# Two norms of eight tiles on GpSimd inside the second attention step, and the last norm's scaling on ScalarE

## The reference

```python
x = x + _L0_gnn_ref(_layernorm(x), adj, ...)
x = x + _L0_ffn_ref(_layernorm(x)[None], ...)[0]
x = x + _L1_gnn_ref(_layernorm(x), adj, ...)
x = x + _L1_ffn_ref(_layernorm(x)[None], ...)[0]

# _L1_gnn_ref: two steps of top-p attention (0.9) and of a fixed graph
for n in range(STEPS):
    A = _top_p_attention(Xa, W1, W2, W3)
    Xf = R @ Xf
    Xa = A @ Xa
    Z = Z + Xf @ U1[n].T + Xa @ U2[n].T
h = X + Z
return (h - mean(h)) / sqrt(var(h) + LN_EPS) * ln_g + ln_b

# _L1_ffn_ref: the routing comes from the mean over all rows, so all rows use the same two experts
logits = mean(x, axis=1) @ Wr + br            # softmax, capacity scale, softmax, top 2, softmax
out = sum over the two experts e of w_e * (gelu(x @ W1[e] + b1[e]) @ W2[e] + b2[e])
return _layer_norm(out + x, gamma, beta)
```

## Time and profile before

| what | value |
| --- | --- |
| median of 3 runs | 904.51 us (904.44 to 907.09) |
| profiled execution | 903.87 us, span 902.1 us |
| VectorE busy | 674.4 us (75%) |
| TensorE busy | 728.7 us (81%) |
| ScalarE busy | 477.1 us (53%) |
| GpSimd busy | 237.0 us (26%) |

### The profile page before, as it was taken

One profiled execution on the slowest core, in us unless ns is written; L12 is line 12 of the kernel. 1 busy time (PEld: TensorE's weight loads), 2 busy tenths in 40 slices (PEclk: granted clock), 3 DMA queues, 4 the chain that ended last, 5 costly groups with the idle time before them and its releaser, 6 DMA issues.

```text
span 902.1 us, 15401 instructions
## 1 busy us (share of the span) xinstructions
PE 728.7 (81%) x5099; PEld 535.5 (59%) x5099; DVE 674.4 (75%) x2305; ACT 477.1 (53%) x707; POOL 237.0 (26%) x489
## 2 busy tenths in 40 slices
PE   4999999859999675999999786967779788775294
PEld 2455555429998443867778476754437576675153
DVE  6758678724444359799871879999899999996768
ACT  4877687115554144465563573849587576602141
POOL 3401330365667007200000142133151341500000
PEclk9999999779999678999999998878788898798588
DMA  8764000076886200000000000000000003001001
GB/s 150 121 94 71 22 22 4 25 214 183 236 234 182 100 1 0 1 2 1 1 2 1 0 2 1 2 1 1 0 1 2 1 2 94 1 1 31 0 4 44
DMA packets 47366, 41.93 MB, mean 46 GB/s; under 512 B 7376, under 2 KB 44112, under 8 KB 47280
## 3 DMA queue, kind: packets, MB, share of 16 engines
q0 software_dynamic: 11456, 14.62, 7.9%
q1 hardware_dynamic: 29488, 19.95, 7.9%
q10 hardware_dynamic: 6336, 6.32, 2.8%
HBM read 39.69 MB, written 9.57 MB: 55 GB/s over the span
## 4 chain that ended last, share of the span: by engine, by line
DVE 37%; PE 17%; issue 5%; ACT 3%; POOLq 1%; DVEq 1%; POOL 1%; ACTq 0%
DVE big L1532 6%; PE bank L1938 4%; PE bank L2033 4%; DVE cand L1451 4%; DVE rm L1306 4%; PE bank L2016 3%; DVE hacc L1446 2%; DVE big L1521 2%; DVE cand L1312 2%; DVE cand L1471 2%; DVE big L1518 2%; DVE top L1466 2%; PE bank L1945 1%; ACT big L1782 1%; PE bank L2195 1%
## 5 line engine op out<-in xcount | busy, mean ns | idle before, releaser
L1782 ACT ACTIVATE big<-bank 128x512 f32<-128x512 f32 x128 | 70.2, 597 | 75.8 <-PE bank L2016 75.8
L2016 PE MATMUL bank<-ident,big 128*128 128x128 f32 x512 | 80.2, 308 | 30.7 <-DVEq L1564 21.4
L1945 PE MATMUL bank<-parts,adjT 128*128 128x128 bf16 x1536 | 92.5, 224 | 5.4 <-DVE xnT L1401 3.4
L1938 PE MATMUL bank<-kk,qq 64*128 64x512 f32 x256 | 78.6, 742 | 21.8 <-ACT big L1752 21.8
L2016 PEld LDWEIGHTS bank<-ident,big 128*128 128x128 f32 x512 | 62.1, 155 | 57.2 <-DVEq L1564 22.5
L1945 PEld LDWEIGHTS bank<-parts,adjT 128*128 128x128 bf16 x1536 | 90.8, 101 | 7.4 <-DVE xnT L1401 3.8
L1752 ACT ACTIVATE big<-bank,negm 128x2048 f32<-128x2048 f32 x32 | 62.6, 1958 | 50.1 <-DVE fsc L1568 40.1
L1532 DVE SCALAR_TENSOR_TENSOR big<-big,st 128x2048 f32<-128x2048 f32 x32 | 75.2, 2388 | 4.8 <-PE bank L2016 4.8
L399 POOL DMA_INDIRECT ys_scratch<-big,parts x62 | 60.0, 967 | 31.5 <-ACT big L759 21.7
L849 PE MATMUL bank<-big,xn 128*128 128x512 f32 x128 | 62.2, 608 | 5.7 <-DVE big L546 5.7
L833 PE MATMUL bank<-xnT 128*128 128x512 f32 x128 | 62.2, 611 | 2.3 <-DVE xnT L535 2.3
(11 more groups left out here) (361 smaller groups left out, 1494.1 us busy)
## 6 DMA issues: line engine op xcount, KB each, us to landing
big<-in_L_ffn_w_dram SPq DMA_DIRECT2D x93, 128.0 KB
big<-in_adj_dram POOLq DMA_DIRECT2D x8, 512.0 KB, 7.5
big<-xs_scratch ACTq DMA_DIRECT2D x31, 132.0 KB
kk<-in_adj_dram POOLq DMA_DIRECT2D x4, 512.0 KB, 8.2
qq<-in_adj_dram POOLq DMA_DIRECT2D x4, 512.0 KB, 10.0
xs_scratch<-hacc SPq DMA_DIRECT2D x9, 132.0 KB
xs_scratch<-hacc ACTq DMA_DIRECT2D x8, 132.0 KB
res<-in_x_dram SPq DMA_DIRECT2D x4, 256.0 KB, 6.9
```

Of the source, the lines that this page charges most:

```text
L1782: nc.scalar.activation(MT[:, 4 * q:4 * q + 4, s * P:(s + 1) * P], bank[:, 5 + q % 2, :].rearrange("p (j i) -> p j i", j=4), ACT.Copy).then ...
L1938: nc.tensor.matmul(bank[:, c, :], qq[lo:lo + DA, (g * G + s) * P:(g * G + s + 1) * P], kk[lo:lo + DA, c * CH:(c + 1) * CH], start=True, st ...
L1945: mm = nc.tensor.matmul(bank[:, b, i * P:(i + 1) * P], adjT[:, jt, t * P:(t + 1) * P], parts[:, k, jt, :], start=(jt == 0 and k == 0), sto ...
L2016: mm = nc.tensor.transpose(bank[:, 5 + q % 2, j * P:(j + 1) * P], mk[:, s, jt * P:(jt + 1) * P], ident[:, :])
```

## The change

- GpSimd gets three helpers. `norm_of` makes mean, variance and inverse root of a slice of tiles, in 21 instructions on 128x4 or 128x8 elements. `first_norm` scales tiles from `h` to `lnu`, multiplies with `lng` and adds into `res`. `second_norm` scales from `res` to `h`.
- They are placed in GpSimd's loop over the groups of the second step: after the search of group 5, `norm_of` and `first_norm` of tiles 0 to 3; after that of group 6, `norm_of` of tiles 0 to 7 (second statistics for 0 to 3, first for 4 to 7) and `first_norm` of 4 to 7; in group 7, `second_norm` of 0 to 3 between the two `after_first`, and after its search `norm_of` and `second_norm` of 4 to 7.
- VectorE takes the statistics of `res` for these tiles with `stats_again` after groups 5 and 6. `two_norms` starts at tile 8 (`EARLY`).
- `lnu` lies in `w_` (`xnT`), not in `mk`; VectorE's wait for all transposes becomes a wait for `less_w` (`sp_done`), the last reader of `w_`. `sums4` gets a buffer of its own.
- TensorE's transposes of the first two quarters of `h` (`turn_h`) and ScalarE's copies of them (`take_h`) move into group 7's round, ahead of the last `flag_sum` and behind the copies of group 6.
- In the last norm ScalarE scales the four tiles of a quarter (Identity with bias and scale), two quarters behind its Gelus. VectorE makes the bias (`nmr`) and does the product with `gam` and the sum into `res` one quarter later (`finish`).

```diff
@@ -1123,15 +1123,17 @@
...
-lnu = mk[:, 1, :].rearrange("p (t d) -> p t d", t=NT)
+lnu = w_
...
-sums4 = r8[:, 8, 2:2 + NC + 1]
+sums4 = sb("sums4", [P, NC + 1])[:, :]
...
 (d_ld, d_ldw, d_xn, d_xT, d_xT_out, d_meanb, d_nm, d_ex, d_w1, d_w2, d_h, d_hid, d_y,
- d_out, d_store) = names("d", "ld", "ldw", "xn", "xT", "xT_out", "meanb", "nm", "ex",
-                         "w1", "w2", "h", "hid", "y", "out", "store")
+ d_out, d_store, d_stat, d_res, d_xn_p, d_nmr, d_yn) = names(
+     "d", "ld", "ldw", "xn", "xT", "xT_out", "meanb", "nm", "ex", "w1", "w2", "h", "hid", "y", "out", "store",
+     "stat", "res", "xn_p", "nmr", "yn")
 FIRST_TILES = (NG - 1) * G
+EARLY = 2 * TPC
@@ -1243,6 +1245,49 @@
...
+        def norm_of(ts):
+            m_, v_, t_, y_, n_ = mean[:, ts], var[:, ts], tmp16[:, ts], rstd[:, ts], newt[:, ts]
+            nc.gpsimd.tensor_tensor(m_, stats[:, ts, 1], stats[:, ts, 4], ALU.add)
+            nc.gpsimd.tensor_tensor(t_, stats[:, ts, 1], stats[:, ts, 4], ALU.subtract)
+            nc.gpsimd.tensor_tensor(v_, stats[:, ts, 2], stats[:, ts, 5], ALU.add)
+            pool.drain()
+            nc.gpsimd.tensor_scalar(m_, m_, 0.5, None, ALU.mult)
+            nc.gpsimd.tensor_scalar(t_, t_, 0.5, None, ALU.mult)
+            nc.gpsimd.tensor_scalar(v_, v_, 1.0 / D, LN_EPS, ALU.mult, ALU.add)
+            pool.drain()
+            nc.gpsimd.tensor_tensor(t_, t_, t_, ALU.mult)
+            pool.drain()
+            nc.gpsimd.tensor_tensor(v_, v_, t_, ALU.add)
+            pool.drain()
+            nc.gpsimd.tensor_scalar(y_.bitcast(I32), v_.bitcast(I32), -0.5, MAGIC, ALU.mult, ALU.add)
+            pool.drain()
+            for _ in range(3):
+                nc.gpsimd.tensor_tensor(n_, v_, y_, ALU.mult)
+                pool.drain()
+                nc.gpsimd.tensor_tensor(n_, n_, y_, ALU.mult)
+                pool.drain()
+                nc.gpsimd.tensor_scalar(n_, n_, -0.5, 1.5, ALU.mult, ALU.add)
+                pool.drain()
+                nc.gpsimd.tensor_tensor(y_, y_, n_, ALU.mult)
+                pool.drain()
+        def first_norm(tiles):
+            for t in tiles:
+                nc.gpsimd.tensor_scalar(lnu[:, t, :], h[:, t, :], mean[:, t:t + 1], rstd[:, t:t + 1],
+                                        ALU.subtract, ALU.mult)
+            pool.drain()
+            for t in tiles:
+                nc.gpsimd.tensor_tensor(lnu[:, t, :], lnu[:, t, :], lng[:, :], ALU.mult)
+            pool.drain()
+            for t in tiles:
+                nc.gpsimd.tensor_tensor(res[:, t, :], res[:, t, :], lnu[:, t, :], ALU.add).then_inc(d_res, 1)
+        def second_norm(tiles):
+            for t in tiles:
+                nc.gpsimd.tensor_scalar(h[:, t, :], res[:, t, :], mean[:, t:t + 1], rstd[:, t:t + 1],
+                                        ALU.subtract, ALU.mult).then_inc(d_xn_p, 1)
         for g in range(NG):
@@ -1251,8 +1296,23 @@
                 continue
             for s in range(G):
                 after_first(g, s)
+                if g == NG - 1 and s == 0:
+                    second_norm(range(0, TPC))
             for s in range(G):
                 after_second(g, s)
+            if g == NG - 3:
+                pool.wait_ge(sp_done, 12)
+                pool.wait_ge(d_stat, TPC)
+                norm_of(slice(0, TPC))
+                first_norm(range(0, TPC))
+            if g == NG - 2:
+                pool.wait_ge(d_stat, 3 * TPC)
+                norm_of(slice(0, EARLY))
+                first_norm(range(TPC, EARLY))
+            if g == NG - 1:
+                pool.wait_ge(d_stat, 4 * TPC)
+                norm_of(slice(TPC, EARLY))
+                second_norm(range(TPC, EARLY))
     @block.vector
@@ -1418,7 +1478,16 @@
             dve.wait_ge(add_done, G * (g + 1))
             dve.wait_ge(rx_added, G * (g + 1))
             for s in range(G):
-                op(nc.vector.bn_stats(stats[:, g * G + s, :], h[:, g * G + s, :]))
+                ins = nc.vector.bn_stats(stats[:, g * G + s, :], h[:, g * G + s, :])
+                if g * G < EARLY:
+                    ins.then_inc(d_stat, 1)
+                else:
+                    op(ins)
+        def stats_again(c):
+            dve.wait_ge(d_res, (c + 1) * TPC)
+            for t in range(c * TPC, (c + 1) * TPC):
+                nc.vector.bn_stats(stats[:, t, :], res[:, t, :]).then_inc(d_stat, 1)
@@ -1613,10 +1682,12 @@
             for k in range(NG - 1):
                 if RXG[k] == g:
                     stats_of(k)
+            if g in (NG - 3, NG - 2):
+                stats_again(g - NG + 3)
         ch.sync()
         dve.wait_ge(c_ldg, 32)
         dve.wait_ge(c_resb, NT)
-        dve.wait_ge(tq_done, 2 * NG * 4 * G)
+        dve.wait_ge(sp_done, 12)
         def two_norms(ts):
@@ -1640,7 +1711,7 @@
                 nc.vector.tensor_scalar(h[:, t, :], res[:, t, :], mean[:, t:t + 1], rstd[:, t:t + 1],
                                         ALU.subtract, ALU.mult).then_inc(d_xn, 1)
-        two_norms(slice(0, FIRST_TILES))
+        two_norms(slice(EARLY, FIRST_TILES))
         add_pv(NG - 1)
         stats_of(NG - 1)
         ch.sync()
@@ -1696,9 +1767,15 @@
...
+        def finish(c):
+            ts = slice(c * TPC, (c + 1) * TPC)
+            dve.wait_ge(d_yn, (c + 1) * TPC)
+            ch.link(nc.vector.tensor_tensor(y[:, ts, :], y[:, ts, :], bcast(gam.unsqueeze(1), [P, TPC, D]),
+                                            ALU.mult))
+            nc.vector.tensor_tensor(res[:, ts, :], res[:, ts, :], y[:, ts, :], ALU.add).then_inc(d_out, 1)
         for c in range(NC):
             ts = slice(c * TPC, (c + 1) * TPC)
-            b3 = [P, TPC, D]
             dve.wait_ge(d_y, c + 1)
@@ -1707,12 +1784,11 @@
             ch.sync()
             mean_var(ch, ts)
             inv_std(ch, ts)
-            for t in range(ts.start, ts.stop):
-                op(nc.vector.tensor_scalar(y[:, t, :], y[:, t, :], mean[:, t:t + 1], rstd[:, t:t + 1],
-                                           ALU.subtract, ALU.mult))
-            ch.sync()
-            ch.link(nc.vector.tensor_tensor(y[:, ts, :], y[:, ts, :], bcast(gam.unsqueeze(1), b3), ALU.mult))
-            nc.vector.tensor_tensor(res[:, ts, :], res[:, ts, :], y[:, ts, :], ALU.add).then_inc(d_out, 1)
+            nc.vector.scalar_tensor_tensor(out=nmr[:, ts], in0=mean[:, ts], scalar=-1.0, in1=rstd[:, ts],
+                                           op0=ALU.mult, op1=ALU.mult).then_inc(d_nmr, 1)
+            if c:
+                finish(c - 1)
+        finish(NC - 1)
...
     @block.scalar
@@ -1846,6 +1922,12 @@
...
+        def take_h(i):
+            a, e = XS[i]
+            act.wait_ge(d_xT, i + 1)
+            nc.scalar.activation(xnT[:, a * P:e * P], bank[:, XB[i], 0:(e - a) * P], ACT.Copy,
+                                 accum_out=sums4[:, i:i + 1]).then_inc(d_xT_out, 1)
@@ -1867,6 +1949,9 @@
             if g:
                 for k in range(4 * G):
                     copy_MT(1, g - 1, k)
+            if g == NG - 1:
+                take_h(0)
+                take_h(1)
             if g + 1 < NG:
@@ -1878,10 +1963,8 @@
                 if g in (2, 3):
                     take_part(g - 2, 1)
                     take_part(g - 2, 2)
-        for i, (a, e) in enumerate(XS):
-            act.wait_ge(d_xT, i + 1)
-            nc.scalar.activation(xnT[:, a * P:e * P], bank[:, XB[i], 0:(e - a) * P], ACT.Copy,
-                                 accum_out=sums4[:, i:i + 1]).then_inc(d_xT_out, 1)
+        for i in range(2, len(XS)):
+            take_h(i)
         act.wait_ge(d_nm, 1)
...
+        def norm(c):
+            act.wait_ge(d_nmr, c + 1)
+            for t in range(c * TPC, (c + 1) * TPC):
+                nc.scalar.activation(y[:, t, :], y[:, t, :], ACT.Identity, bias=nmr[:, t:t + 1],
+                                     scale=rstd[:, t:t + 1]).then_inc(d_yn, 1)
         act.wait_ge(d_w1, 4)
...
                     act.wait_ge(d_y, c - 1)
                 nc.scalar.activation(hid[:, c % 2, u, :], bank[:, v % 4, :], ACT.Gelu,
                                      bias=db1[:, u // HCD, u % HCD:u % HCD + 1]).then_inc(d_hid, 1)
+            if c >= 2:
+                norm(c - 2)
+        for c in range(NC - 2, NC):
+            norm(c)
     @block.tensor
     def _(pe):
@@ -2130,6 +2223,18 @@
...
+        def turn_h(i):
+            a, e = XS[i]
+            if i == len(XS) - 1:
+                pe.wait_ge(add_done, NT)
+            for t in range(a, e):
+                if t < EARLY:
+                    pe.wait_ge(d_xn_p, t + 1)
+                else:
+                    pe.wait_ge(d_xn, t + 1 - EARLY)
+                mm = nc.tensor.transpose(bank[:, XB[i], (t - a) * P:(t - a + 1) * P], h[:, t, :], ident[:, :])
+            mm.then_inc(d_xT, 1)
@@ -2171,16 +2276,15 @@
             for k in range(1, NG, 2):
                 if RXG[k] == g:
                     rx(k)
+            if g == NG - 1:
+                pe.wait_ge(p_ready, 2 * NG * G)
```

(11 more changed lines are left out.)

## The result

The changed kernel took 896.12 us in the median of 4 runs (894.77 to 897.17), beside 904.98 for the kernel before; the ratio is 0.9891 with a 95% interval of 0.987 to 0.9912. It is faster by 1.1%, 8 to 12 us. In a second set of runs, beside others of before, it was 893.86 against 905.36, ratio 0.9884 (0.9861 to 0.9907). Forecast were 893.8 and a range of 890 to 899.

A forecast was written before the change was run, and what follows sets the result against it. The prediction took VectorE, busy 37% of the span, as the bound, with TensorE's products next after group 7. Its terms -13.3 + 1.6 + 1.5 - 0.2 gave -10.4 us: 893.8 us, range 890 to 899.

The forecast's parts named there:

- The end of the second step: Between group 7's end and its `add_pv`, moving tiles 0 to 7 off VectorE removes 13.3 of 26.3 us.
- TensorE is late next: After group 7, VectorE finishes at 826.7 and then waits for TensorE's products, ending at 827.2; 0.5 us of saving is lost.
- `stats_again`, +1.6: After groups 5 and 6, four extra `bn_stats` on VectorE each time, with nothing to hide them, cost 1.6 us.
- VectorE behind GpSimd, +1.5: In the groups, three or four collisions of 0.4 to 0.8 us with GpSimd's large instructions cost VectorE 1.5 us.
- Rival A: GpSimd hardly disturbs VectorE and the search has slack: -11.9 us, giving 892.3; chance 0.20.
- Rival C: `first_norm` instructions over 0.8 us delay GpSimd's threshold search; VectorE waits 2 to 4 us in groups 6 and 7: 896 to 901; chance 0.15.
- cost nothing: Group 7's threshold search starts 4 us late on GpSimd, but 4.3 us of cover and ScalarE absorb it: no cost.
- The early transposes and copies, nothing: Transposes and copies of tiles 0 to 7 fit TensorE's 5.17 us idle before the last flag sum: no cost or gain.
- The last norm, -0.2: In the last two quarters, ScalarE's scaling saves 0.2 us, between -0.6 and +0.6, because TensorE paces the earlier quarters.
- The whole last feed-forward, unchanged in themselves.: Behind `add_pv` of group 7, the routing and last feed-forward keep their lengths and merely come earlier.
- Rival B: GpSimd's added work, 26.6 us, blocks VectorE in full: 918.9 us, slower once over 11.9 us block; chance 0.05.
- rival D: Identity scalings between the Gelus make ScalarE reload its table, two or three exposed loads of 1.3 us: 896.5 to 898; chance 0.07.

The follow-up runs named there:

- after: The changed kernel in its first set of runs and the trace from it; 896.12 us for 904.98 before, ratio 0.9891.
- after_again: The changed kernel run again with no edit, in a second set of runs with its own trace; 893.86 us for 905.36 before, ratio 0.9884.
- skip_third: The changed kernel without VectorE's two norms of tiles 8 to 11 (output wrong there), on another chip; ratio 0.989 to before.
- pool_more: The changed kernel with each of GpSimd's eight first scalings made two more times into unused tiles, on another chip; ratio 0.9963 to before.
- pe_warm: The changed kernel with 36 and 22 unused bf16 products filling two idle stretches of TensorE; ratio 0.9835 to before.
- warm_table2: pe_warm plus one tiny Gelu on ScalarE behind the routing's last Exp; 890.06 us, ratio 0.9834 to before (0.9826 on another chip, as warm_table).
- warm_all: The warm_table2 kernel plus 22 unused bf16 products on TensorE in front of the last flag sum; 890.61 us, ratio 0.985 to before.

## Why the prediction was right, point by point

- **The end of the second step, -13.3 us.** Measured -13.7 (after) and -12.9 (after_again). The step "TensorE is late next" held: skip_third shows VectorE idling for it. It is level with VectorE rather than 0.5 us behind it: before's transposes took 6.35 us up to the product, after's 5.97, after_again's 6.76. What I didn't foresee is that the stretch has two lengths with the clock.
- **`stats_again`, +1.6.** Its rows are 0.86 us for four, 0.77 and 0.77 with overlap. As said, with nothing to hide it.
- **VectorE behind GpSimd, +1.5.** This term was mis-sized: groups 5 to 7 grew by 1.99 us in all, so about 0.45 for the exclusion. I had counted three or four collisions of 0.4 to 0.8 us; there were three larger ones of 0.1 to 0.23. The row that I leaned on, 1.02 us in the earlier trace rows, is one short instruction that started behind a run of additions with no gap and ended with the last of them (365.42 and 365.40 us); here the large instructions fell into MAX8 and MATCH_REPLACE, as the prediction itself said, and pool_more prices such collisions at a tenth of GpSimd's large time. Rival A, without this term, was the better account of the mechanism. Of the signs that I named, the groups' growth of 3 us came out at 2.0 and the single instructions of 0.4 to 1 us didn't come.
- **GpSimd's own time.** The scaling by pointers, which no row of before showed, takes 0.80 us and not 0.455: 16 of them, 5.5 us more on GpSimd. Rival C asked for 0.8 us in each of the twelve instructions of `first_norm`; only the four scalings reached it, the products and additions stayed at 0.455, and C didn't come. But it was near. `after_first` of group 7 began at 769.49, 7.7 us later than in the earlier trace rows (VectorE itself ran 3.5 us later by then), ScalarE waited for it, `second_norm` took 3.2 us for 1.8, the search stood behind VectorE twice and not once, and of the 4.3 us of cover 1.8 were left. That "cost nothing" held with so little to spare was luck in part: in pool_more what goes beyond the cover comes through one to one.
- **The early transposes and copies, nothing.** Right: they lie in TensorE's idle time, and the flags' wait of 5.09 us is as long as the 5.17 in the earlier trace rows.
- **The last norm, -0.2.** Measured -0.39 in every trace that has it. The third quarter took 5.91 us for the 6.03 that I worked out and the fourth 7.78 for 7.85; TensorE's pace hides the rest, as said.
- **"The whole last feed-forward, unchanged in themselves."** Not quite: 12.64 us to the first quarter became 12.97 and 13.58. The three kernels without the moved norms show 12.43 to 12.81; with them, and without fills, it is 12.86 (pool_more) to 13.62 (skip_third). It goes against the stretch behind group 7: the kernels with 13.1 to 13.2 us there have 13.6 here, those with 13.9 have 12.9 or 13.0, so the two together are 26.7 to 26.9 each time. The sum is 39.5 us before, so 12.6 to 12.8 us are gained in both together, where 13.3 and nothing were forecast. pe_warm shows that the clock prices this stretch; why the change lengthens it, with other idle times of TensorE ahead of it, the runs don't settle.
- **Rival B** (VectorE blocked for over 11.9 us) and **rival D** (tables) are out. ScalarE's table load stands ahead of the first Gelu alone; the Identity scalings between the Gelus have none; there are four loads in the trace, as before.
- **The sum.** -10.4 forecast; -10.96 between before and after_again, whose groups 3 and 4 are alike; -8.9 and -11.5 in the medians of two sets of runs. That the sum is so near is in part luck: VectorE behind GpSimd cost 1.05 us less than its term and the last norm gave 0.2 more, while the stretch behind group 7 gave 0.4 less and the up products took 0.3 more. The 2.3 us by which the first median missed 893.8 are of the size of the wandering in group 3 and at the up products, and the trace of the second set, whose median is 893.86, has the shorter lengths in both; the runs without a trace can't be told apart this way. Nor can the times tell the forecast (893.8) from rival A (892.3); only the traces do.

## What to carry to other kernels

Ask first why a buffer sits where it does: moving one alias and one wait gave over half of this gain, the eight moved tiles the smaller part. Before moving more work off an engine, find the other engine's end that comes next, here TensorE's product, which was level with VectorE after the change, since past it nothing is gained. And before explaining a difference of 1 to 3 us between two traces, cut both at the same landmarks, also ahead of the change, and look at the granted clock where they part.

## What the runs showed of the hardware

- TensorE's clock cost 2.2 to 2.8 us behind idle times: the first up products ran at a granted 0.50 after 6.3 us of idling, and at 1.00 when 36 and 22 unused bf16 products filled that gap and the 8.9 us one ahead of it (10.8 us for 13.0 and 13.6). In pe_warm and warm_table2 the clock fell to 0.50 during the fill and was at 1.00 again before the up products. Where a fill ended with 0.35 and 2.15 idle us around a flag sum (warm_all), the next products began at 0.52; where it ended with 1.51 idle us (warm_table), at 1.00.
- The same kernel had group 3 at 35.38 and at 37.89 us in two executions, with the clock at 1.00 or part of the time at 0.50 during the `less_w` products.
- On GpSimd a 128x128 `tensor_scalar` with two per-partition scalars took 0.80 us, a `tensor_tensor` of that size 0.455.
- VectorE's MAX8 and MATCH_REPLACE ran at their usual lengths beside GpSimd's large instructions (but for one of 1.29 us for 1.21 in pool_more); short scalings, scans and two-operand instructions were held up by 0.1 to 0.35 us each.
- A 128x1 instruction of GpSimd beside VectorE's long ones took 2.1 to 2.4 us in place of 0.2 to 0.3 (2.41 and 2.21 in after, 2.27 and 2.08 in pool_more).
